# A feed-forward block with a conditioned layer norm: the norm by pairs of tiles, x split half an item ahead

## The chip, the cores and the metric

One core of one Trainium2 chip. Times are device microseconds of one execution. Engines by their names in the profile: PE is TensorE (PEld its weight loads), DVE VectorE, ACT ScalarE, POOL GpSimd, SP SyncE, whose queue issues the DMAs.

## The reference

```python
xr = x.reshape(4, 1024, 8, 128)                                  # x: (4, 1024, 1024) f32
h = gelu(einsum('btel,elf->btef', xr, W1) + b1)                  # W1: (8, 128, 512), exact gelu
y = (einsum('btef,efl->btel', h, W2) + b2).reshape(4, 1024, 1024)  # W2: (8, 512, 128)
eo = silu(emb) @ emb_W + emb_b                                   # emb: (4, 1024), emb_W: (1024, 2048)
scale, shift = split(eo[:, None, :], 2, axis=-1)
hn = layernorm(y, ln_g, ln_b) * (1.0 + scale) + shift            # over the 1024 features
out = x + silu(hn) @ out_W + out_b                               # out_W: (1024, 1024)
```

## The kernel before

Every matmul of weight is made of three in fp32r: each operand is split into a rounded part (`_hi`) and the rest (`_lo`), and hi x hi, lo x hi and hi x lo are added up in PSUM. For each such operand one engine rounds (a cast) and one subtracts.

**Stage A** runs over 32 items (`ORDER`, line 32): a feature group g of 8 and a token tile t of 1024 tokens. Groups 0 to 5 go through all four tiles each, groups 6 and 7 tile by tile. An item has four chunks c of 128 hidden features; m = 4n + c counts the chunks. `first(m)` (line 672) multiplies W1's chunk with x (x comes transposed as `xT`), six matmuls of 512 columns; ScalarE applies gelu into `g_raw`; ScalarE (c = 3, 0) or VectorE (c = 1, 2) rounds to `g_hi`, VectorE subtracts to `g_lo` (`split_gelu`, line 528); `second(m)` (line 686) adds W2's chunk into the item's y. TensorE's order is written out by hand: for each m, `first(m + 2)`, then `second(m)` (lines 733 to 769). The ring of two PSUM slots (`USES`, `SLOT`, `take`) is shared with small matmuls: eight embeddings of the condition (`embed`), their turning, and three steps of window 0's norm.

x of item n+1 is rounded by ScalarE at the start of item n (`round_x`) and its rest made by VectorE at c = 1 (`rest_x`, line 523), one chunk ahead of its first use at c = 2. The raw weights of both stages are rounded by ScalarE (`round_raw`, line 408) and subtracted by GpSimd (`low`, line 347). ScalarE stages y to SBUF (`stage_y`), SP stores it to `y_scratch`; VectorE adds it up over the groups into `acc` (`add_up`, line 540), from which the mean comes by one matmul with `ones`. SP's order in an item (lines 280 to 312): raw weights, emb_W, x of item n+2, then the store of y.

**Stage B** runs over 8 windows of 512 tokens. A window has four tiles of 128 tokens; a tile is 8 groups of six matmuls (`project`, line 771). Meanwhile the next window is normed (`window`, line 610): mean by a matmul of `acc`, centring on VectorE, squares on ScalarE, a tree of sums on VectorE, `variance` (four one-column fp32 matmuls), root on ScalarE, reciprocal of 4 columns, `spread` (four transposes) back over the features, the multiplication, silu on ScalarE with scale and bias, rounding and rest. `finish(q)` adds the tile's product to `res`, to which GpSimd has added out_b; SP stores it. Window 0 is normed inside stage A's last items, mostly on GpSimd (lines 362 to 376), and its silu stands behind stage A's last gelu (lines 467 to 478, and VectorE's lines 595 to 603).

Of the kernel before, what the change touches and what calls it, by code (L numbers as in the profile page):

```python
# [5 lines left out]
P = 128  # L6
# [5 lines left out]
BANK = 512  # L12
# [3 lines left out]
def cond_ffn_program(nc, x, xT, vectors, W1, W2, emb_W, out_W, out_b, out):  # L16
# [7 lines left out]
    TB = BANK  # L24
    NB = B * T // TB
    SB = TB // P
# [5 lines left out]
    ORDER = [(g, t) for g in range(G - 2) for t in range(NT)] + [(g, t) for t in range(NT) for g in (G - 2, G - 1)]  # L32
# [5 lines left out]
    Y0_ITEM = ITEM_OF[G - 1, 0]  # L38


    LOADS = [("W", 0), ("W", 1), ("W", 2), ("O", 0), ("O", 1), ("W", 3), ("O", 2), ("O", 3), ("W", 4), ("O", 4),
             ("W", 5), ("O", 5), ("W", 6), ("O", 6), ("W", 7), ("O", 7)]
    PREP_ITEM = [None, 0, 1, 2, 3, 5, 6, 7, 9, 11, 13, 15, 17, 19, 21, 22]
    LOAD_OF = {u: j for j, u in enumerate(LOADS)}
    PREP_AT = {n: j for j, n in enumerate(PREP_ITEM) if n is not None}
    EMB_ITEM = [5 + 2 * r for r in range(KE)]
    EMB_AT = {(n, 2): r for r, n in enumerate(EMB_ITEM)}
    TURN_AT = (21, 2)
    Y0_MEAN_AT = (Y0_ITEM + 2, 0)
    Y0_SQ_AT = [(Y0_ITEM + 2, 3), (Y0_ITEM + 3, 1), (Y0_ITEM + 3, 2), (Y0_ITEM + 4, 0)]  # L50
    Y0_VAR_AT = (Y0_ITEM + 4, 3)
    Y0_RSTD_AT = (Y0_ITEM + 5, 1)


    USES = [("S", 0), ("S", 1)]
    for m in range(M):
        at = divmod(m, C)
        if at in EMB_AT:
            USES.append(("E", EMB_AT[at]))
        if at == TURN_AT:  # L60
            USES.append(("F", 0))
        if at == Y0_MEAN_AT:
            USES.append(("M", 0))
        if at == Y0_VAR_AT:
            USES.append(("V", 0))
        if at == Y0_RSTD_AT:
            USES.append(("R", 0))
        if m + 2 < M:
            USES.append(("S", m + 2))
    SLOT = {u: j % 2 for j, u in enumerate(USES)}  # L70
    EARLIER = {u: USES[j - 2] for j, u in enumerate(USES) if j >= 2}
# [5 lines left out]

    y_scratch = nc.dram_tensor("y_scratch", [NB, P, G, TB], F32, kind="Internal").ap()

# [9 lines left out]
    with ExitStack() as ctx:  # L89
# [14 lines left out]
        acc = at("acc", [P, NT, TA], 64 * KB)  # L104
        S0 = 80 * KB
        ident = at("ident", [P, P], S0)
        ones = at("ones", [P, P], S0 + 512)
        cols = at("cols", [P, ROWS], S0 + 1024)
        stat = at("stat", [P, TB], S0 + 1536)
        emb_rows = at("emb_rows", [P, BANK], S0 + 3584)  # L110
        sq_sum = emb_rows
        cond_silu = at("cond_silu", [P, KE, 32], S0 + 5632)
        emb = at("emb", [P, NE, B], S0 + 6656)
        mod_a = at("mod_a", [P, B, G], S0 + 6912)
        mod_c = at("mod_c", [P, B, G], S0 + 7040)
        mod_t = at("mod_t", [P, B, G], S0 + 7168)
        eps = at("eps", [P, 1], S0 + 7296)
        std = at("std", [P, SB], S0 + 7328)
        rstd = at("rstd", [P, SB], S0 + 7360)
        R0 = S0 + 15 * 512  # L120


        yb0 = at("yb0", [P, G, TB], R0)
        emb_raw = at("emb_raw", [P, 2 * D], R0 + 16 * KB)
        wraw = at("wraw", [P, 2, 2 * FF], R0 + 24 * KB)
        squares = at("squares", [P, 4, TB], R0 + 24 * KB)
        xT_raw = at("xT_raw", [P, 2, TA], R0 + 32 * KB)
        xT_hi = at("xT_hi", [P, 2, TA], R0 + 40 * KB, F32R)
        xT_lo = at("xT_lo", [P, 2, TA], R0 + 48 * KB, F32R)
        g_raw = at("g_raw", [P, 2, TA], R0 + 56 * KB)  # L130
        g_hi = at("g_hi", [P, 2, TA], R0 + 64 * KB, F32R)
        g_lo = at("g_lo", [P, 2, TA], R0 + 72 * KB, F32R)
        W = at("W", [P, 3, 4, FF], R0 + 80 * KB, F32R)
        y_stage = at("y_stage", [P, 2, TA], R0 + 104 * KB)
        out_b_all = at("out_b_all", [P, D], R0 + 112 * KB)

        yb1 = at("yb1", [P, G, TB], R0 + 16 * KB)
        s_hi0 = at("s_hi0", [P, G, TB], R0 + 32 * KB, F32R)
        s_lo0 = at("s_lo0", [P, G, TB], R0 + 48 * KB, F32R)
        sq0 = at("sq0", [P, G, TB], R0 + 48 * KB)  # L140
        s_hi1 = at("s_hi1", [P, G, TB], R0 + 64 * KB, F32R)
        s_lo1 = at("s_lo1", [P, G, TB], R0 + 80 * KB, F32R)
        sq1 = at("sq1", [P, G, TB], R0 + 80 * KB)
        res = at("res", [P, 4, D], R0 + 96 * KB)
        yb = (yb0, yb1)
        s_hi = (s_hi0, s_hi1)
        s_lo = (s_lo0, s_lo1)
        sq = (sq0, sq1)
# [4 lines left out]
        ident_ready = sem("ident_ready")  # L153
        ones_ready = sem("ones_ready")
# [3 lines left out]
        w_hi_done = sem("w_hi_done")  # L158
        w_split0 = sem("w_split0")
# [6 lines left out]
        aw_hi_done = sem("aw_hi_done")  # L166
        pw_split = sem("pw_split")
# [694 lines left out]
```

## Time and profile before

| | us |
|---|---|
| median of 3 runs (790.39 to 793.78) | 792.9 |
| the profiled execution | 794.72 |
| its span, first to last instruction | 792.9 |
| PE busy | 751.7 (95%) |
| DVE busy | 489.3 (62%) |
| ACT busy | 418.1 (53%) |
| POOL busy | 165.6 (21%) |
| mean granted clock of TensorE | 0.982 |

Busy time is the time in which an engine has an instruction under way. The chain of the work that ended last goes to 78% through PE, to 11% through DVE and to 5% through ACT.

### The profile page before, as it was taken

Reading aid. Unit: us, or ns where it says so; the run is one execution under the profiler, and the core shown is the slowest. Engines: PE = TensorE matmul, PEld = TensorE weight load, DVE = VectorE, ACT = ScalarE, POOL = GpSimd, SP = SyncE. Lnnn points to the kernel's source line nnn. Section 1 sums busy time; section 2 is a strip of 40 time slices with the busy share of each in tenths; the row PEclk is TensorE's granted clock in tenths of the full one; section 3 lists DMA queues with packets and bytes.
Section 4 is the critical chain, followed back from the end, with each engine's and each line's share of the span. In section 5 each row is a group of like instructions: output and inputs, shape, how many; then the busy total and the mean of one; then the engine's idle time right before and its main releaser. Section 6 shows DMA issues by size and latency. Waiting matters only on the chain.

```text
span 792.9 us, 8091 instructions
## 1 busy us (share of the span) xinstructions
PE 751.7 (95%) x3252; PEld 597.4 (75%) x3252; DVE 489.3 (62%) x393; ACT 418.1 (53%) x413; POOL 165.6 (21%) x91
## 2 busy tenths in 40 slices
PE   6999999999999999996877999999999999999998
PEld 5777777777787777674655867888788888878886
DVE  6778778877877877766498256355444535554211
ACT  6877877777877777665652143334250423425000
POOL 1221211110101200335372112212221221121210
PEclk9999999999999999998989999999999999999999
DMA  5333554335543222511072243252423325212221
GB/s 214 119 120 134 169 175 153 136 137 186 186 158 109 107 77 83 213 53 54 26 292 106 80 139 127 107 212 89 176 107 136 129 107 212 99 61 107 106 80 53
DMA packets 33268, 101.75 MB, mean 128 GB/s; under 512 B 3024, under 2 KB 7120, under 8 KB 31056
## 3 DMA queue, kind: packets, MB, share of 16 engines
q1 hardware_dynamic: 32560, 100.73, 35.3%
q10 hardware_dynamic: 672, 0.52, 0.2%
q8 instruction: 25, 0.41, 0.2%
q14 instruction: 11, 0.09, 0.0%
HBM read 67.69 MB, written 33.55 MB: 128 GB/s over the span
## 4 chain that ended last, share of the span: by engine, by line
PE 78%; DVE 11%; ACT 5%; issue 4%; DMA 2%; POOL 1%; SPq 0%; ACTq 0%; DVEq 0%; POOLq 0%
PE psum L778 39%; PE psum L682 17%; PE psum L696 17%; DVE g_lo L537 4%; DVE xT_lo L525 2%; DVE g_hi L535 2%; PE psum L789 1%; ACT g_raw L400 1%; DMA xT_raw<-in_xT 1%; PE psum L711 1%; PE psum L822 1%; PE psum L704 1%; DVE s_hi L599 1%; ACT yb L470 1%; ACT xT_hi L392 1%
## 5 line engine op out<-in xcount | busy, mean ns | idle before, releaser
L537 DVE TENSOR_TENSOR g_lo<-g_raw,g_hi 128x1024 fp32r<-128x1024 f32 x128 | 178.3, 1393 | 74.1 <-ACT g_hi L406 71.9
L400 ACT ACTIVATE g_raw<-psum,cols 128x1024 f32<-128x1024 f32 x128 | 142.9, 1117 | 71.1 <-PE psum L682 69.8
L778 PE MATMUL psum<-oW_hi,s_hi 128*128 128x512 f32 x496 | 159.7, 403 | 3.7 <-DVE res L608 1.9
L778 PE MATMUL psum<-oW_hi,s_lo 128*128 128x512 f32 x496 | 155.2, 394 | 1.6 <-DVE s_lo L601 1.6
L778 PE MATMUL psum<-oW_lo,s_hi 128*128 128x512 f32 x496 | 154.3, 393 | 0.0
L682 PE MATMUL psum<-xT_hi,W 128*128 128x512 f32 x508 | 140.0, 398 | 5.0 <-ACT g_raw L400 2.6
L696 PE MATMUL psum<-g_hi,W 128*128 128x512 f32 x512 | 140.2, 396 | 0.0
L381 POOL TENSOR_TENSOR res<-res,out_b_all 128x1024 f32<-128x1024 f32 x32 | 79.0, 2472 | 281.6 <-DMA res<-in_x 281.6
L682 PEld LDWEIGHTS psum<-xT_hi,W 128*128 128x128 f32 x508 | 95.7, 191 | 33.4 <-issue 9.3
L696 PEld LDWEIGHTS psum<-g_hi,W 128*128 128x128 f32 x512 | 97.6, 191 | 22.1 <-DVE g_hi L535 0.5
L778 PEld LDWEIGHTS psum<-oW_hi,s_hi 128*128 128x128 f32 x496 | 93.4, 191 | 26.8 <-issue 4.1
L778 PEld LDWEIGHTS psum<-oW_hi,s_lo 128*128 128x128 f32 x496 | 94.2, 190 | 21.9 <-DVE s_lo L601 2.0
L778 PEld LDWEIGHTS psum<-oW_lo,s_hi 128*128 128x128 f32 x496 | 94.1, 190 | 20.1
L682 PE MATMUL psum<-xT_lo,W 128*128 128x512 f32 x254 | 82.4, 406 | 13.4 <-DVE xT_lo L525 13.4
L608 DVE TENSOR_TENSOR res<-psum,res 128x1024 f32<-128x1024 f32 x31 | 37.7, 1220 | 88.3 <-PE psum L778 88.3
L487 ACT ACTIVATE sq<-yb 128x2048 f32<-128x2048 f32 x14 | 26.9, 1919 | 120.8 <-DVE yb L617 120.8
L696 PE MATMUL psum<-g_lo,W 128*128 128x512 f32 x256 | 80.2, 395 | 2.2 <-DVE g_lo L537 2.2
L406 ACT CAST g_hi<-g_raw 128x1024 fp32r<-128x1024 f32 x64 | 67.2, 1050 | 22.4 <-PE psum L696 22.3
L470 ACT ACTIVATE yb<-yb,mod_c,mod_a 128x512 f32<-128x512 f32 x64 | 46.9, 804 | 47.4 <-DVE yb L633 47.4
L682 PEld LDWEIGHTS psum<-xT_lo,W 128*128 128x128 f32 x254 | 46.4, 191 | 31.2 <-DVE xT_lo L525 22.4
L535 DVE CAST g_hi<-g_raw 128x1024 fp32r<-128x1024 f32 x64 | 47.2, 738 | 22.7 <-ACT g_raw L400 17.0
L696 PEld LDWEIGHTS psum<-g_lo,W 128*128 128x128 f32 x256 | 48.5, 190 | 13.8 <-DVE g_lo L537 3.5
(83 smaller groups left out, 554.3 us busy)
## 6 DMA issues: line engine op xcount, KB each, us to landing
y_scratch<-y_stage SPq DMA_DIRECT2D x32, 512.0 KB, 2.9
res<-in_x SPq DMA_DIRECT2D x32, 512.0 KB, 3.9
xT_raw<-in_xT SPq DMA_DIRECT2D x31, 512.0 KB, 4.4
out<-res SPq DMA_DIRECT2D x31, 512.0 KB, 2.8
yb<-y_scratch SPq DMA_DIRECT2D x7, 2048.0 KB, 9.5
emb_raw<-in_emb_W SPq DMA_DIRECT2D x8, 1024.0 KB, 7.7
wraw<-in_out_W SPq DMA_DIRECT2D x16, 256.0 KB, 3.7
wraw<-in_W SPq DMA_DIRECT2D x14, 256.0 KB, 3.6
```

Of the source, the lines that this page charges most:

```text
L381: nc.gpsimd.tensor_tensor(res[:, q % 4], res[:, q % 4], out_b_all[:], ALU.add).then_inc(res_biased, 1)
L400: nc.scalar.activation(g_raw[:, m % 2], ring(("S", m)), ACT.Gelu, bias=cols[:, R_B1 + k:R_B1 + k + 1]).then_inc(gelu_done, 1)
L406: nc.scalar.copy(g_hi[:, m % 2], g_raw[:, m % 2]).then_inc(ghi_act, 1)
L470: return nc.scalar.activation(yb[s][:, g], yb[s][:, g], ACT.Silu, scale=mod_a[:, b, g:g + 1], bias=mod_c[:, b, g:g + 1])
L487: nc.scalar.activation(sq[s][:, half], yb[s][:, half], ACT.Square).then_inc(squared, 1)
L525: nc.vector.tensor_tensor(xT_lo[:, n % 2], xT_raw[:, n % 2], xT_hi[:, n % 2].bitcast(F32), ALU.subtract).then_inc(xlo_done, 1)
L535: nc.vector.tensor_copy(g_hi[:, m % 2], g_raw[:, m % 2]).then_inc(ghi_dve, 1)
L537: nc.vector.tensor_tensor(g_lo[:, m % 2], g_raw[:, m % 2], g_hi[:, m % 2].bitcast(F32), ALU.subtract).then_inc(glo_done, 1)
L608: nc.vector.tensor_tensor(res[:, q % 4], proj(q), res[:, q % 4], ALU.add).then_inc(out_ready, 1)
L682: mm = nc.tensor.matmul(ps[:, half], W[:, g % 3, w, cut], v[:, n % 2, half], start=(k == 0), stop=(k == 2))
L696: mm = nc.tensor.matmul(y_psum(n)[:, half], W[:, g % 3, w, cut], v[:, m % 2, half], start=(c == 0 and k == 0), stop=(c == C - 1 and k == 2))
L778: mm = nc.tensor.matmul(proj(q)[:, half], v[:, g, cut], w[:, g, half], start=(g == 0 and k == 0), stop=(g == G - 1 and k == 2))
```

## The change

- The norm works on pairs of token tiles (256 tokens, `NP` = 16 pairs) in place of windows of 512, two pairs ahead, with three y buffers (`load_y`, 1 MB each).
- `acc`, `add_up`, `variance` and `spread` are gone. Mean and variance come from a tree of sums over the groups of y or of its squares, made on VectorE; the sum is split high and low (`sum_hi`, `sum_lo`) and summed over the partitions by two fp32r matmuls with a 128x128 of 1/D, which leave it in every partition (`row_sum`). The reciprocal then has 256 columns.
- Pair 0's norm is spread by hand over items 24 to 30 of stage A, on VectorE and ScalarE. Its silu is computed as v(1 + tanh v) with v half the argument (`halve_y0`, `tanh_y0`, `silu_y0`). Pair 1's mean is in item 31.
- Items: groups 5, 6 and 7 are now the ones that go tile by tile, so tile 0's y is complete with item 22. Four weight slots (`WS`) in place of three.
- x of item n+2 is rounded at c = 2 and its rest made at c = 3 of item n. SP issues x's load first in an item; the y store stands right before it.
- Both steps of the weights' split are VectorE's (`split_raw`); GpSimd has only `ident` and the `res` additions left.
- The small matmuls of stage A use a bank of the free y slot (`small`) in place of the ring.
- Two fp32 matmuls on zeros run on TensorE before the first weights are there.

```diff
-    ORDER = [(g, t) for g in range(G - 2) for t in range(NT)] + [(g, t) for t in range(NT) for g in (G - 2, G - 1)]
+    LATE = range(G - 3, G)
+    ORDER = [(g, t) for g in range(G - 3) for t in range(NT)] + [(g, t) for t in range(NT) for g in LATE]
...
+    SPLIT_ITEM = [None, 0, 1, 2, 3, 5, 7, 8, 9, 11, 12, 13, 14, 15, 17, 19]
+    EMB_ITEM = [4 + 2 * r for r in range(KE)]
+    TURN_ITEM = 20
+    Y0_MEAN_AT = (25, 1)
+    Y0_VAR_AT = (27, 1)
+    Y1_MEAN_AT = (31, 3)
...
         def _(sp):
+                if n + 2 < N:
+                    sp.wait_ge(xlo_done, n + 1)
+                    load_x(n + 2)
...
                 if n == Y0_ITEM + 1:
+                    sp.wait_ge(emb_chunk, KE)
                     for s in range(2):
+                        sp.wait_ge(y_stored[s], 16 * len(range(s, Y0_ITEM + 1, 2)))
+                    for p in range(3):
+                        load_y(p)
...
         def _(act):
+                if c == 2 and n + 2 < N:
+                    round_x(n + 2)
+                if (n, c) == (28, 0):
+                    root(0, total[:])
+                    nc.scalar.preload_act_table(ACT.Gelu)
                 if m + 2 < M:
                     gelu(m + 2)
+                if (n, c) == (25, 3):
+                    square(0, 0)
+                if (n, c) == (26, 0):
+                    square(0, 1)
+                if (n, c) == (28, 3):
+                    act.wait_ge(mod_step, 7)
+                    halve_y0(0)
+                    halve_y0(1)
+                if (n, c) == (29, 0):
+                    halve_y0(2)
+                    halve_y0(3)
+                if (n, c) == (29, 1):
+                    tanh_y0(0)
+                if (n, c) == (29, 3):
+                    round_y0(0)
+                    halve_y0(4)
+                    halve_y0(5)
+                if (n, c) == (30, 0):
+                    halve_y0(6)
+                    halve_y0(7)
+                    tanh_y0(1)
+                if (n, c) == (30, 2):
+                    round_y0(1)
...
         def _(dve):
+            def split_raw(j, h):
+                raw = wraw[:, j % 2, half]
+                nc.vector.tensor_copy(hi, raw).then_inc(w_rounded, 1)
+                nc.vector.tensor_tensor(lo, raw, hi.bitcast(F32), ALU.subtract).then_inc(w_split, 1)
...
+                if c == 3 and n + 2 < N:
+                    rest_x(n + 2)
+                if m + 2 < M:
+                    split_gelu(m + 2)
+                if c in (0, 2) and n in SPLIT_AT:
+                    split_raw(SPLIT_AT[n], c // 2)
...
+            for i in range(NP):
+                p, ahead = i + 1, i + 2
+                if p < NP:
+                    invert(p, rstd_ps)
+                    norm(p, 0, rstd_ps)
+                    norm(p, 1, rstd_ps)
                 if i > 0:
+                    finish(2 * i - 1)
+                if ahead < NP:
+                    mean_sum_first(ahead)
+                    mean_sum_rest(ahead)
+                    mean_split_up(ahead)
+                if p < NP:
+                    rest_s(p, 0)
+                if ahead < NP:
+                    centre(ahead, 0, mean_ps)
+                    centre(ahead, 1, mean_ps)
+                if p < NP:
+                    rest_s(p, 1)
+                finish(2 * i)
+                if ahead < NP:
+                    var_sum_first(ahead)
+                    var_sum_rest(ahead)
+                    var_split_up(ahead)
...
         def _(pe):
+            def row_sum(ps):
+                nc.tensor.matmul(ps, ones_r[:], sum_hi[:], start=True, stop=False)
+                return nc.tensor.matmul(ps, ones_r[:], sum_lo[:], start=False, stop=True)
...
+            pe.wait_ge(emb_copied, 1)
+            for j in range(2):
+                nc.tensor.matmul(psum[:, 7], emb_rows[:, 0:P], emb_rows[:], start=True, stop=True)
...
+            for i in range(NP):
+                ahead = i + 2
+                for t in range(2):
...
+                        project(q, g)
+                        if i == 0:
+                            if (t, g) == (0, 4):
+                                var_of(1)
+                            if (t, g) == (1, 1):
+                                mean_of(ahead)
+                        elif ahead < NP:
+                            if (t, g) == (0, 0) and i == 1:
+                                var_of(2)
+                            if (t, g) == (0, 6):
+                                mean_of(ahead)
+                            if (t, g) == (1, 6):
+                                var_of(ahead)
```

## Rows read from the trace of the kernel before

**Rows 1.** Three stretches; stretch: length, busy us (instructions), clock, DMA share, GB/s.
```profile
110.40:317.50 207.10, 205.08 (x907) 159.85 (x906) 163.07 (x155) 158.89 (x159) 25.35 (x16) 1.00 0.40 138
317.50:424.30 106.80, 83.83 (x313) 62.87 (x312) 76.14 (x58) 61.41 (x63) 50.46 (x27) 0.90 0.33 123
489.90:720.30 230.40, 230.40 (x1032) 188.14 (x1031) 114.12 (x71) 81.31 (x75) 48.18 (x21) 1.00 0.35 128
```

**Rows 2.** Timeline of ACT: stagings of items 0, 26 and 31; start, duration.
```profile
23.16 1.12 ACT L423 ACTIVATE y_stage<-psum,cols 128x1024 f32<-128x1024 f32 x1
...
327.58 1.11 ACT L423 ACTIVATE y_stage<-psum,cols 128x1024 f32<-128x1024 f32 x1 [0.24 <-PE psum L696]
...
406.30 1.09 ACT L423 ACTIVATE y_stage<-psum,cols 128x1024 f32<-128x1024 f32 x1
```

**Rows 3.** The chain in stage A, 110 to 162 us; start, duration, what.
```profile
116.70 1.36 PE psum L696 x6
118.06 1.36 PE psum L682 x6
...
123.50 1.00 PE psum L704 x8
```

**Rows 4.** The chain in stage B, 510 us on.
```profile
517.16 0.86 PE psum L822 x2
...
528.94 1.03 PE psum L711 x8
...
535.53 0.44 PE psum L717 x4
535.97 27.23 PE psum L778 x120
```

**Rows 5.** Waits: waiter, line, waited for: us in total, times, longest.
```profile
PE psum L682 <- DVE xT_lo L525: 13.4, 11, 4.4
```

**Rows 6.** Timeline of POOL and DVE near 27 us.
```profile
26.81 1.29 POOL L348 TENSOR_TENSOR W<-wraw,W 128x512 fp32r<-128x512 f32 x1 [2.86 <-ACT W L415]
...
26.99 2.20 DVE L537 TENSOR_TENSOR g_lo<-g_raw,g_hi 128x1024 fp32r<-128x1024 f32 x1
...
29.11 1.21 DVE L525 TENSOR_TENSOR xT_lo<-xT_raw,xT_hi 128x1024 fp32r<-128x1024 f32 x1
```

**Rows 7.** Timeline of the start: chunk 2's gelu, and item 1's low part.
```profile
13.01 1.11 ACT L400 ACTIVATE g_raw<-psum,cols 128x1024 f32<-128x1024 f32 x1
...
18.28 0.73 PE L682 MATMUL psum<-xT_lo,W 128*128 128x512 f32 x2 [0.91 <-DVE xT_lo L525]
```

**Rows 8.** Groups by line and shape; count, busy us, mean ns, idle before.
```profile
L406 ACT CAST g_hi<-g_raw 128x1024 fp32r<-128x1024 f32 x64 | 67.2, 1050 | 22.4 <-PE psum L696 22.3
...
L535 DVE CAST g_hi<-g_raw 128x1024 fp32r<-128x1024 f32 x64 | 47.2, 738 | 22.7 <-ACT g_raw L400 17.0 <-PE psum L696 5.6
...
L548 DVE SCALAR_TENSOR_TENSOR acc<-psum,cols,acc 128x1024 f32<-128x1024 f32 x28 | 35.7, 1277 | 0.0
...
L488 ACT ACT_TABLE_LOAD x7 | 9.0, 1283 | 0.1
...
L415 ACT CAST W<-wraw 128x512 fp32r<-128x512 f32 x14 | 8.6, 614 | 0.0
...
L624 DVE TENSOR_TENSOR stat<-sq 128x512 f32<-128x512 f32 x7 | 4.8, 692 | 0.2
...
L627 DVE RECIPROCAL rstd<-std 128x4 f32<-128x4 f32 x7 | 1.2, 178 | 11.4 <-ACT std L490 11.4
...
L510 DVE CAST W<-wraw 128x512 fp32r<-128x512 f32 x2 | 0.8, 424 | 2.7 <-DMA wraw<-in_W 2.7
```

**Rows 9.** SP's timeline at 227 us, landings of `xT_raw`, and the page's DMA issues.
```profile
227.04 0.43 SPq L256 DMA_DIRECT2D xT_raw<-in_xT  x1
...
DMA to landing us min/median/max: 3.6/4.1/9.1
...
yb<-y_scratch SPq DMA_DIRECT2D x7, 2048.0 KB, 9.5
```

**Rows 10.** The chain's last matmuls.
```profile
778.76 10.89 PE psum L789 x48
```

More of the change, by code:

```diff
@@ L126, in cond_ffn_program @@
[L126 to L144, printed above, removed]
@@ new lines, in _ @@
+            for q in range(QN):
+                if q < QN - 1:
+                    sp.wait_ge(out_ready, q + 1)
+                    sp.dma_start(out_rows[q], res[:, q % 4]).then_inc(out_stored[q % 4], 16)
+                else:
+                    for h in range(2):
+                        half = slice(h * BANK, (h + 1) * BANK)
+                        sp.wait_ge(out_ready, QN + h)
+                        sp.dma_start(out_rows[q, :, half], res[:, q % 4, half]).then_inc(out_stored[q % 4], 16)
+                if q % 2 == 0 and q // 2 + 4 < NP:
+                    p = q // 2 + 4
+                    sp.wait_ge(slo_done, 2 * (p - 3) + 2)
+                    load_y(p)
+                if q >= 1 and q + 3 < QN:
+                    sp.wait_ge(out_stored[(q - 1) % 4], 16 * ((q - 1) // 4 + 1))
+                    load_res(q + 3)
@@ new lines, in centre, with var_sum_first @@
+            def centre(p, h, mean):
+                dve.wait_ge(mean_done, p + 1)
+                part = yb[p % 3][:, half_of(h)]
+                nc.vector.tensor_tensor(part, part, mean.unsqueeze(1).to_broadcast([P, HG, TP]), ALU.subtract
+                                        ).then_inc(centred, 1)
+            def var_sum_first(p):
+                dve.wait_ge(squared, 2 * p + 2)
+                nc.vector.tensor_tensor(sq[:, 0:4], sq[:, 0:4], sq[:, 4:8], ALU.add).then_inc(var_tree, 1)
@@ new lines, in invert, with norm, silu_y0 @@
+            def invert(p, rstd):
+                dve.wait_ge(std_done, p + 1)
+                nc.vector.reciprocal(rstd, std[:]).then_inc(rstd_done, 1)
+            def norm(p, h, rstd):
+                dve.wait_ge(rstd_done, p + 1)
+                part = yb[p % 3][:, half_of(h)]
+                nc.vector.tensor_tensor(part, part, rstd.unsqueeze(1).to_broadcast([P, HG, TP]), ALU.mult
+                                        ).then_inc(normed, 1)
+            def silu_y0(h):
+                dve.wait_ge(y0_tanh, h + 1)
+                part = yb0[:, half_of(h)]
+                nc.vector.scalar_tensor_tensor(part, sq[:, half_of(h)], 1.0, part, ALU.add, ALU.mult
+                                               ).then_inc(y0_silu, 1)
@@ new lines, in _ @@
+                if (n, c) == (28, 3):
+                    norm(0, 1, total[:])
+                if (n, c) == (29, 2):
+                    silu_y0(0)
+                if (n, c) == (30, 0):
+                    rest_s(0, 0)
+                if (n, c) == (30, 1):
+                    silu_y0(1)
+                if (n, c) == (30, 3):
+                    rest_s(0, 1)
+                if (n, c) == (31, 0):
+                    mean_sum_first(1)
+                if (n, c) == (31, 1):
+                    mean_sum_rest(1)
+                    mean_split_up(1)
```

666 lines of the change are left out of this document (281 added, 385 removed).

## The prediction

> **What bounds the kernel now.** I read the stretches first: TensorE's busy time in each, and its clock. From 110 to 317 us the PE is busy 205.08 of 207.10 us, and from 490 to 720 us all of 230.40 us; from 317.5 to 424.3 us it is busy for 83.8 of 106.8 us at a granted clock of 0.90 [rows 1]. So TensorE is the bound except in the middle. The chain gives its pace: six matmuls, one call of `first` or `second` or one group of `project`, take 1.36 us in stage A [rows 3], and 120 of stage B take 27.23 us, 0.2269 us each, so 1.361 us for six [rows 4]. The kernel has 256 sixes in stage A and 256 in stage B: 696.8 us of the 792.9 us span. The rest, 96 us, is what can be won.
>
> Where it lies: stage A's items. An item is eight sixes, 10.89 us. From the staging of item 0 (23.16 us) to that of item 26 (327.58 us) an item took 304.42/26 = 11.71 us; the last five took 78.7 us where 51.7 us of matmuls stand [rows 2]. That is 21 us in the first part (8 of it for the condition's eight embeddings, 1.00 us each [rows 3]) and 27 us in the second. 10 us lie before item 0's staging (ten sixes are 13.6 us), and 38 us behind item 31's: 16.3 for seven windows of norm matmuls, 3.3 behind the last matmul, 18.6 of stalls at the start of stage B. The waits show the cause in the first part: TensorE for `xT_lo` 13.4 us [rows 5]; and where GpSimd runs at the same time, a `g_lo` of VectorE takes 2.20 us instead of the 1.22 that a subtraction of this size takes by itself [rows 6]. That delays `xT_lo`, which stands one chunk ahead of its use. In stage B a window of four tiles has 192 project matmuls (43.57 us) and 0.86 + 1.03 + 0.44 = 2.33 us of norm matmuls [rows 4].
>
> **The change, part by part.** T is the time at which TensorE begins an item; the order in an item is first, second, four times, 1.36 us each.
>
> *Start.* Two warm-up matmuls and a reordered VectorE. Before, the fifth call of `first` got its low part at 18.28 us [rows 7]. After, VectorE does for it: the split of chunk 2 (gelu ready at 14.12 us [rows 7], cast 0.74, low part 1.22), then half a weight split (0.42 + 0.69 [rows 8]), then `rest_x(1)` (1.22): 18.4 us. The warmed clock wins about 1 us earlier, but this wait swallows it. I take item 0 staged at 23.3 us; -1 to +1.
>
> *VectorE in stage A.* Gone: `add_up` (1.28 an item) [rows 8] and GpSimd's 30 half splits, with the 2.20 us cases. New: both halves of each weight split on VectorE. A full item is now 4 x 1.22 + 2 x 0.74 + 1.22 (`rest_x`) + 2 x (0.42 + 0.69) = 9.8 us, and 0.69 for an embedding, against 10.89 (11.9 with embedding): it fits. Order matters too: chunk 4n+4's low part ends at T+11.1, the half split at T+12.2, `rest_x(n+2)` at T+13.3 and chunk 4n+5's cast and low part at T+14.0 and T+15.2; TensorE wants these at T+14.96 and T+15.9. 0.7 us are left, the thinnest cover of the change; where embedding and split meet (items 8, 12, 14) I book 0.3 us in all. ScalarE loses 30 casts of 0.61 us and has 4 x 1.12 + 2 x 1.05 + 1.05 + 1.12 = 8.7 of 10.89 us.
>
> *x half an item ahead.* `xT_hi` and `xT_lo` of item n+2 are made in item n, so TensorE's 13.4 us of waits go. What is late next is the load: issued at about T+1.6 (behind the y store, now ahead of the weight and embedding loads), wanted by ScalarE at T+6.6. 5.0 us against a landing of 4.1 us in the median and 9.1 at most; the 9.1 goes with an issue at 227.04 us behind weights and emb_W [rows 9]. So nothing in an ordinary item. In item 23, however, the three 1 MB loads of y are new on this queue: 2 MB took 9.5 us [rows 9], so 3 MB some 14 us at that rate, perhaps 11, from T+4; they end at T(24)+4 to +8, with the y store and x of item 24 behind them. x comes 2 to 6 us late, ScalarE and VectorE have 1 to 2 us in hand there. I take 2 us lost; 0 to 5.
>
> *Stage A's sum.* From item 0's staging to the end of A stand 246 sixes, 334.8 us. Embeddings 8 x 1.15 = 9.2 (1.00 each plus a part of a refilled weight load; 8.0 at least). The turn 0.7. Three row sums 0.9.
>
> *Pair 0's norm in items 24 to 30* replaces the tail in which `second`, the POOL chain and window 0 waited for each other. TensorE no longer waits on it; only its load on ScalarE and VectorE counts. 24 to 27 add at most 3.1 us of VectorE a item, which had 3.4 free. Item 28 adds on ScalarE two table loads (1.28 each [rows 8]) and a root (0.5) before a gelu: the gelu ends at T+5.4, wanted at T+5.44. Items 28 to 30 then add 8 scalings of 256 columns (0.40 each, from 0.61 for 512 and 1.05 for 1024), two tanh and two roundings (1.05 each). Item 28 is 12.5 us of ScalarE and item 29 12.4 us, 3.1 us over two items' TensorE time; and a scaling stands behind `normed`, a rounding behind `silu_y0`, with the next gelu queued behind both. Followed, chunk by chunk, that costs TensorE 3 to 4.5 us. I take 3.8; 1 to 8.
>
> A ends at 23.3 + 334.8 + 9.2 + 0.7 + 0.9 + 0.3 + 2 + 3.8 = 375.0 us. Before, its last staging began at 406.3 us, and stalls went on behind it: the slow stretch reaches to 424.3 us [rows 1, 2].
>
> *Stage B.* 256 sixes, 348.4 us. Row sums: two fp32r matmuls of 256 columns take the place of mean, variance and spread. No row has one. From below: half of 0.2269 each, 0.23 us a sum; from above, the fp32 mean of before, 512 columns in 0.86 us: 256 columns twice are 0.43 each at its pace if both passes are needed, 0.57 with a restart of the next weight load. I take 0.30, near the fp32r row, since `ones_r` and the sums are fp32r. 29 of them in B: 8.7 us (6.7 to 16.5), where the seven windows had 16.3.
>
> Does the rest hide? VectorE a pair (22.4 us of TensorE): 2 norm, 2 centre, 2 `finish`, 2 `rest_s` and 2 first tree steps of 1024 columns, 12.3 us; two second steps (0.69), two third (0.42), two split-ups (0.3 + 0.42), 3.7 us; the reciprocal. It now has 256 columns, the rows only 4, 0.178 us [rows 8]; at one column a cycle it is 0.42. Beyond that it is bounded above by the 1024-column row, 1.22; I take 0.5. Sum 16.5 us, plus about 2 us of meeting GpSimd's two res adds. It fits with 4 us over. In order: invert and norms end at 2 us of the window, `finish` 3.3, the mean's split 7, TensorE asks at 9.5; variance's split at 18, asked for at 20.9. Hidden. In the first window they are tight (asked for at 6.8 us after B's start, ready at 6.7): 1.5 us booked, 0 to 4.
>
> The Trainium skill speaks against my reciprocal: "VectorE: DVE Perf Modes" (the 8-slice pipeline) says that it repeats its divide 8 times per element. By that 256 columns would be an estimated 2.3 us, the window of VectorE 18.3 us, still hidden, and the sum 2 us more, in the first window.
>
> **The sum.** 375.0 + 348.4 + 8.7 + 1.5 and the tail behind the last matmul, 792.93 - 789.65 = 3.3 us [rows 10], is a span of 736.9 us. The profiled execution ran 794.72 us for a span of 792.93, 1.8 more, and lies 1.8 above the median of 792.9: in terms of the median the two cancel. **737 us.**
>
> **Rivals.** (1) *VectorE or ScalarE becomes the bound of a full item in A.* The 0.7 us of cover is gone if each semaphore step costs a little more than I read. Eleven split items at 1 us each, four late items at 2 more: 737 + 11 + 8 = 756. For: the thinnest margin in the change. Against: back-to-back VectorE instructions start about 0.08 us before the last ends. 0.12.
> (2) *B's norm chain is late for TensorE's fixed places.* If reciprocal and meetings with GpSimd take 4 us more, the mean is late at (0, 6) by 1 us in each of 14 windows: 737 + 14 = 751. For: one chain, in order, through three engines. Against: 2.5 us spare. 0.10.
> (3) *Tanh isn't with Gelu in the loaded table.* A load there and back before each of two tanh, 2 x 2 x 1.28 = 5.1 us on ScalarE in items 29 and 30, where it has nothing over: 742. The diff puts no load there, and every load in the trace of before stands at a `preload` line; that is against it. The Trainium skill, "ScalarE: Activation LUTs" (table sets), lists tanh with exp and with sigmoid, not with gelu, and would have it so. 0.08.
> (4) *Slower: x lands late in every item.* If 1 KB pieces of the y store and the shorter lead make each x land as late as the worst before, 9.1 us, it is 4.1 us behind its 5.0 us, 2.4 beyond what ScalarE has over, 30 times: 737 + 72 = 809. It beats the gain from a landing of some 8.5 us on. Against: x is now issued before the big loads, and 2.5 MB an item move at 210 GB/s. 0.03.
> (5) *Nothing in the tail is won*: the pair norm stalls `second` as before, 27 us in the last items return: 764. 0.04.
> The forecast holds the remaining 0.63.
>
> **Range.** All unknowns good (no stalls, sums at 0.23, embeddings 1.00): 737 - 7.6 - 2.2 - 1.2 = 726; two of them good, 729. Above, sums at 0.57 and rivals 2 and 1: to 756. 729 to 756. Faster by over 0.5% (about what can be told from no change here) 0.95, the same 0.02, slower 0.03.
>
> **What would show it.** Stagings of item 0 and 27 some 307 us apart or less (27 x 10.89 + 9.2 + 2 + 1.6); no wait for `xT_lo`; all `g_lo` near 1.22 us; GpSimd idle before its res adds; a clock of 1.00 from 20 us on; ScalarE's waits in items 28 to 30 for `normed` and `silu_y0`, with TensorE waiting for g_raw or `g_lo` there; B's windows of two tiles at 22.4 us. Wrong it would be if x's landing exceeds 6 us in many items, if a row sum takes over 0.5 us, or if VectorE fills over 95% of an item.

## The result, and the profile after

| | before | after |
|---|---|---|
| median, us | 792.6 | 750.8 (749.7 to 754.2) |
| profiled execution, us | 794.7 | 751.7 |
| its span | 792.9 | 749.9 |
| ratio to before, 95% interval | | 0.948 (0.944 to 0.952) |

The kernel before ran again in the same round, hence 792.6 and not 792.9. The change makes the kernel 5% faster, and its time is 14 us above the forecast of 737, inside the range of 729 to 756. The page of the kernel after gives busy us, share of the span and instructions of each engine:

```profile
PE 729.4 (97%) x3208; PEld 588.0 (78%) x3208; DVE 549.6 (73%) x618; ACT 457.6 (61%) x502; POOL 78.5 (10%) x38
```

VectorE has 60 us more work than before, GpSimd 87 us less, TensorE 22 us less. Where the forecast was missed shows in the stretches. The columns are those of [rows 1]: length, busy us of each engine with its instructions, clock, DMA share, GB/s.

```profile
110.00:290.00 180.00, 179.88 (x806) 143.38 (x805) 136.54 (x159) 134.66 (x126) 0.00 (x0) 1.00 0.48 161
290.00:340.00 50.00, 45.41 (x188) 36.73 (x187) 35.33 (x39) 35.47 (x35) 0.00 (x0) 0.93 0.23 78
340.00:380.00 40.00, 37.66 (x156) 27.84 (x154) 32.07 (x30) 34.77 (x39) 0.00 (x0) 1.00 0.24 73
380.00:430.00 50.00, 43.26 (x185) 34.93 (x186) 43.43 (x47) 26.96 (x34) 12.04 (x5) 0.97 0.35 131
490.00:700.00 210.00, 210.00 (x944) 174.37 (x943) 160.67 (x180) 105.47 (x138) 44.99 (x20) 1.00 0.38 136
```

In the first row 0.1 of 180 us are idle, before it was 2.0 of 207 [rows 1]. Stage B from 490 us on is full too. What is lost lies between 290 and 430 us: 13.7 us without a matmul, and two stretches with a granted clock below 1.00, the first of which no engine's load explains: VectorE is 71% busy from 290 to 340 us. From 380 to 430 us it is 87% busy, part of it in operations that GpSimd stretches (below). The waits (waiter, line, waited for: us in total, times, longest) name who ends it:

```profile
PE psum L753 <- DVE sum_lo L548: 7.8, 4, 3.5
...
PE psum L753 <- DVE sum_lo L571: 3.8, 2, 2.2
...
PE psum L713 <- DVE xT_lo L498: 1.6, 1, 1.6
```

L753 is the row sum on TensorE, L548 and L571 the low part of the mean's and of the variance's sum. The row of `xT_lo` is what is left of the 13.4 us in [rows 5]; it is item 1's at the start. The timeline of item 25, VectorE first, then TensorE (start, duration, line, operation, tile, and in brackets the idle time before it and who ended it):

```profile
296.76 0.69 DVE L508 CAST g_hi<-g_raw 128x1024 fp32r<-128x1024 f32 x1
297.49 1.23 DVE L510 TENSOR_TENSOR g_lo<-g_raw,g_hi 128x1024 fp32r<-128x1024 f32 x1
298.63 0.29 DVE L546 CAST sum_hi<-total 128x256 fp32r<-128x256 f32 x1
298.95 0.42 DVE L548 TENSOR_TENSOR sum_lo<-total,sum_hi 128x256 fp32r<-128x256 f32 x1
```

```profile
296.47 0.61 PE L729 MATMUL psum<-g_lo,W 128*128 128x512 f32 x2
299.52 0.55 PE L753 MATMUL psum<-sum_hi,ones_r 128*128 128x256 f32 x1 [2.44 <-DVE sum_lo L548]
299.87 0.41 PE L754 MATMUL psum<-sum_lo,ones_r 128*128 128x256 f32 x1
300.08 1.91 PE L713 MATMUL psum<-xT_hi,W 128*128 128x512 f32 x4
```

TensorE arrives at the row sum at 297.1 us. VectorE has the split of the sum behind the cast and low part of a gelu that TensorE wants only after the row sum, and finishes it at 299.37. TensorE stands for 2.44 us, and the four matmuls behind the stop take 1.91 us where the usual is 1.07: half pace, the 1.2 GHz level. The same comes at (27, 1) with 2.16 us and at (31, 3) with 3.48 us.

The row sum in stage B's first window stops for 1.61 us too (395.15 us). There VectorE's split takes six times its 0.42 us, while GpSimd works from 392.45 us on:

```profile
392.55 2.54 DVE L571 TENSOR_TENSOR sum_lo<-total,sum_hi 128x256 fp32r<-128x256 f32 x1
```

The terms of the sum beside the trace, in us. The last column is the version e5_gate, told below.

| | forecast | after | e5_gate |
|---|---|---|---|
| item 0 staged | 23.3 | 22.0 | 22.3 |
| from there to item 24's staging | 271.3 | 272.4 | 272.5 |
| from there to the end of A | 80.4 | 91.0 | 80.1 |
| stage B up to the last matmul | 358.6 | 361.3 | 358.4 |
| tail | 3.3 | 3.2 | 3.2 |
| span | 736.9 | 749.9 | 736.4 |

### The profile page after: what moved, and what is told of

It reads as the page before. It is cut to its first block, busy times and chain, and to the rows that moved or that the text cites. A ratio compares the mean times of both kernels' runs of the same rounds, so it can differ in the third digit from the quotient of the medians.

```text
span 749.9 us, 8247 instructions
## 1 busy us (share of the span) xinstructions
PE 729.4 (97%) x3208; PEld 588.0 (78%) x3208; DVE 549.6 (73%) x618; ACT 457.6 (61%) x502; POOL 78.5 (10%) x38
## 4 chain that ended last, share of the span: by engine, by line
PE 84%; DVE 7%; ACT 5%; issue 2%; DMA 1%; SPq 0%; ACTq 0%; DVEq 0%
PE psum L818 42%; PE psum L713 19%; PE psum L729 19%; DVE g_lo L510 2%; ACT g_raw L347 2%; PE psum L830 1%; ACT g_hi L353 1%; PE psum L739 1%; PE psum L753 1%; DMA xT_raw<-in_xT 1%; DVE yb L581 1%; DVE g_hi L508 1%; DMA cols<-in_vectors 1%; ACT y_stage L360 1%; PE psum L754 1%
## 5 line engine op out<-in xcount | busy, mean ns | idle before, releaser
L510 DVE TENSOR_TENSOR g_lo<-g_raw,g_hi 128x1024 fp32r<-128x1024 f32 x128 | 156.8, 1225 | 82.9 <-ACT g_hi L353 80.4
L818 PE MATMUL psum<-oW_hi,s_hi 128*128 128x512 f32 x496 | 153.7, 391 | 0.0
L818 PE MATMUL psum<-oW_hi,s_lo 128*128 128x512 f32 x496 | 153.2, 390 | 0.0
L818 PEld LDWEIGHTS psum<-oW_hi,s_hi 128*128 128x128 f32 x496 | 91.6, 189 | 17.3
L713 PE MATMUL psum<-xT_lo,W 128*128 128x512 f32 x254 | 79.3, 394 | 1.6 <-DVE xT_lo L498 1.6
L729 PE MATMUL psum<-g_lo,W 128*128 128x512 f32 x256 | 80.1, 394 | 0.1
L451 ACT ACTIVATE yb<-yb,mod_c,mod_a 128x256 f32<-128x256 f32 x120 | 62.4, 590 | 26.8 <-DVE yb L581 26.8
L576 DVE RECIPROCAL psum<-std 128x256 f32<-128x256 f32 x15 | 26.4, 1761 | 52.9 <-ACT std L377 52.9
L377 ACT ACTIVATE std<-psum,eps 128x256 f32<-128x256 f32 x15 | 7.2, 477 | 93.5 <-PE psum L754 93.5
L365 ACT ACTIVATE sq<-yb 128x1024 f32<-128x1024 f32 x32 | 34.0, 1063 | 40.6 <-DVE yb L554 39.6
L713 PEld LDWEIGHTS psum<-xT_lo,W 128*128 128x128 f32 x254 | 48.2, 190 | 12.1 <-DVE xT_lo L498 2.0
```

Of the source, the lines that this page charges most:

```text
L365: nc.scalar.activation(sq[:, half_of(h)], yb[p % 3][:, half_of(h)], ACT.Square).then_inc(squared, 1)
L451: nc.scalar.activation(yb[p % 3][:, g], yb[p % 3][:, g], ACT.Silu, scale=mod_a[:, b, g:g + 1], bias=mod_c[:, b, g:g + 1]).then_inc(silu_do ...
L510: nc.vector.tensor_tensor(g_lo[:, m % 2], g_raw[:, m % 2], g_hi[:, m % 2].bitcast(F32), ALU.subtract).then_inc(glo_done, 1)
L576: nc.vector.reciprocal(rstd, std[:]).then_inc(rstd_done, 1)
L713: mm = nc.tensor.matmul(ring(m)[:, half], W[:, g % WS, w, cut], v[:, n % 2, half], start=(k == 0), stop=(k == 2))
L729: mm = nc.tensor.matmul(y_psum(n)[:, half], W[:, g % WS, w, cut], v[:, m % 2, half], start=(c == 0 and k == 0), stop=(c == C - 1 and k == 2))
```

## Experiments

**Is it the place of the row sums?** The theory at this point was that both row sums of pair 0 stand one chunk too early in TensorE's order, and that pair 1's mean is begun too late on VectorE. The rival was the clock: the stops are short, and what counts is the half pace behind them. Four kernels ran beside each other, the first of them the changed kernel once more.

> The changed kernel once more, as the measure for the runs beside it: 750 us, with TensorE's three stops in front of the row sums of items 25, 27 and 31 (2.4, 2.2 and 3.5 us) where they were.

Measured: 749.2 us (747.2 to 751.9), ratio 0.945 (0.941 to 0.949). The three stops are there with 2.57 us and about the same two others, but in this execution TensorE kept its pace behind the first two:

```profile
300.83 0.36 PE L753 MATMUL psum<-sum_hi,ones_r 128*128 128x256 f32 x1 [2.57 <-DVE sum_lo L548]
301.02 0.28 PE L754 MATMUL psum<-sum_lo,ones_r 128*128 128x256 f32 x1
301.14 1.09 PE L713 MATMUL psum<-xT_hi,W 128*128 128x512 f32 x4
```

So the same stop lowers the granted clock in one execution and not in another (from 290 to 340 us it is 1.00 here, 0.93 in the profile after). From item 24's to item 28's staging this execution takes 52.4 us, the other 55.4: so the half pace behind the first two stops is worth 2.9 us. Up to item 31's staging 2.3 of it are left (89.3 against 91.6), because here the half pace behind the third stop begins at the row sum itself.

Then the places alone:

```diff
-    Y0_MEAN_AT = (25, 1)
-    Y0_VAR_AT = (27, 1)
+    Y0_MEAN_AT = (25, 2)
+    Y0_VAR_AT = (27, 2)
```

> The row sums of pair 0's mean and variance stand one chunk later in TensorE's order, (25, 2) and (27, 2). Theory: the stops come only from the fixed place, which asks for sum_lo 13.6 us after item 24's start while VectorE has it after 16.1. One chunk later it is asked for at 16.3. Items 25 and 27 fall from 15.2 and 15.1 us to 11.3, so the time falls by 7 to 8 us, to 742 to 743. Rival: ScalarE and VectorE have no time to spare in items 24 to 28, and the stop is only where that shows; then the same time is lost behind it, at g_hi or g_lo, and less than 2 us come back (748 or more).

Measured: 742.8 us (742.1 to 743.2), ratio 0.936 (0.934 to 0.939), 6.5 us below a0_again, near the theory's 7 to 8 and far from the recorded rival's less than 2. Both stops are gone: the stagings of items 24 and 28 are 47.2 us apart, where a0_again has 52.4 and the profile after 55.4. One `sum_lo` stop is left in stage A, that of (31, 3), again 3.48 us.

Next, pair 1's mean tree half an item earlier on VectorE as well:

```diff
+                if (n, c) == (30, 2):
+                    mean_sum_first(1)
                 if (n, c) == (30, 3):
                     rest_s(0, 1)
-                if (n, c) == (31, 0):
-                    mean_sum_first(1)
-                if (n, c) == (31, 1):
                     mean_sum_rest(1)
+                if (n, c) == (31, 0):
                     mean_split_up(1)
```

> Beside e1's edit, pair 1's sums for the mean are made one to three chunks earlier on VectorE, so that sum_lo is there when TensorE reaches (31, 3). Theory: the 3.5 us stop there and about 1.5 us at half clock behind it go too, and stage B's first row sums, which hang on the same chain, wait less: 12 to 15 us below the changed kernel, 735 to 738. Rival: items 30 and 31 are bound by ScalarE's gelus behind the halved and tanh work, and VectorE's tree now pushes g_lo back by its own length; then no more than 1 us below e1.

Measured: 746.4 us (745.3 to 746.9), ratio 0.941 (0.938 to 0.943), slower than e1_places by 3.7. The stop at (31, 3) did go, and stage B began at 375.35 us instead of 379.28. But the next row sum, pair 1's variance in the first window of B, was then late, by more than was won: in e1_places it had not waited. The timelines of GpSimd, VectorE and TensorE in this kernel:

```profile
376.94 10.95 POOL L328 TENSOR_TENSOR res<-res,out_b_all 128x1024 f32<-128x1024 f32 x4 [375.49 <-DMA res<-in_x]
```

```profile
380.46 2.76 DVE L563 TENSOR_TENSOR sq<-sq 128x512 f32<-128x512 f32 x1
383.26 2.44 DVE L565 TENSOR_TENSOR total<-sq 128x256 f32<-128x256 f32 x1
385.73 2.31 DVE L569 CAST sum_hi<-total 128x256 fp32r<-128x256 f32 x1
388.08 0.42 DVE L571 TENSOR_TENSOR sum_lo<-total,sum_hi 128x256 fp32r<-128x256 f32 x1
```

```profile
388.56 0.58 PE L753 MATMUL psum<-sum_hi,ones_r 128*128 128x256 f32 x1 [6.23 <-DVE sum_lo L571]
```

GpSimd's four additions of x and bias run back to back for 10.95 us. Within them a VectorE addition of 512 columns takes 2.76 us (0.69 elsewhere), one of 256 columns 2.44 (0.42), a cast of 256 columns 2.31 (0.29): each sits out one GpSimd addition, and the first one behind GpSimd's end is back at 0.42. In e1_places the four additions came two and two (from 377.74 and from 385.22 us), and the small steps of the tree, 383.63 to 385.56 us, passed between them. So a third mechanism was at work that neither theory nor rival held.

The clock rival was tried by giving TensorE unread matmuls ahead of the row sums of the changed kernel (10, 9 and 15 of them, on a free bank), so that it is busy until `sum_lo` is there:

```diff
                 if (n, c) == Y0_MEAN_AT:
                     pe.wait_ge(y_staged, n)
                     pe.wait_ge(ones_ready, 1)
+                    fill(n, 10)
                     pe.wait_ge(mean_split, 2)
```

> Before each of the three row sums TensorE runs matmuls whose results nobody reads (10, 9 and 15 of 512 columns, 2.3, 2.0 and 3.4 us), about as long as it stood still there. Theory: the stop itself costs 8.1 us and remains; but behind each stop a call of six matmuls took 1.9 to 2.5 us in place of 1.36, with a granted clock of 0.91 to 0.98 in the stretches there, some 4 us in all. With the engine busy the clock stays at its upper level and these 4 us come back: 746. Rival: the slow matmuls behind a stop are data or weight waits, not the clock; then nothing comes back, 750 or a little more.

Measured: 751.3 us (750.9 to 752.1), ratio 0.947 (0.945 to 0.950): nothing came back. The pace behind all three places is full in its profile, and from item 24's to item 31's staging it takes 88.5 us, 0.8 less than a0_again, which lost its pace at the third stop alone. But in B's first window the variance was late by 5.2 us, at a clock of 0.83 from 380 to 400 us: GpSimd's additions fell on the split of the sum, a cast of 2.31 us (0.29) and a subtraction of 2.44 (0.42). Matmuls without an idle time ahead of them kept the full pace, which speaks against the recorded rival (data or weights late behind a stop), but in one execution only. What the fillers alone are worth can't be read from this run; removing the stops is worth 6.5 us, and that is the way that pays.

**Does GpSimd hold VectorE?** The third mechanism got a run of its own. To e3_both comes one thing: GpSimd's additions wait.

```diff
+                if q == 0:
+                    pool.wait_ge(mean_split, 6)
+                if q == 2:
+                    pool.wait_ge(var_split, 6)
```

> The two earlier places and the earlier mean tree as in e3_both, and GpSimd's four res additions before stage B are held until VectorE has split the mean's sum (first two) and the variance's sum (last two) of pair 1. Theory (a GpSimd addition holds VectorE's SBUF operations, up to 2.76 us for a 128x512 addition instead of 0.69): with GpSimd idle during the variance tree of pair 1, its operations return to 0.69, 0.42 and 0.29 us, the wait of 6.2 us on sum_lo goes to about 0 to 1 us, TensorE keeps 2.4 GHz behind it, and the span is 736 to 738 us, 6 to 8 below e3_both. Rival (VectorE is slow there for a reason of its own, such as its queue of psum evictions): the wait stays near 6 us and the span near 745. Second rival (the held additions come late for the first windows of B, which need res): the wait goes, but TensorE or ScalarE waits 2 to 5 us for res later, span 740 to 743.

Measured: 738.6 us (738.1 to 739.1), ratio 0.932 (0.929 to 0.935), span 736.4. VectorE's tree in this kernel, and the row sum that waits for it:

```profile
379.62 0.69 DVE L567 TENSOR_TENSOR sq<-sq 128x512 f32<-128x512 f32 x1
380.35 0.43 DVE L569 TENSOR_TENSOR total<-sq 128x256 f32<-128x256 f32 x1
380.81 0.29 DVE L573 CAST sum_hi<-total 128x256 fp32r<-128x256 f32 x1
381.13 0.43 DVE L575 TENSOR_TENSOR sum_lo<-total,sum_hi 128x256 fp32r<-128x256 f32 x1
```

```profile
381.67 0.33 PE L757 MATMUL psum<-sum_hi,ones_r 128*128 128x256 f32 x1
```

All four are at their usual length, and the row sum has no idle time before it. The only difference to e3_both is that GpSimd stands still, so the hold by GpSimd is shown. Its price here is 7.8 us between the medians and 8.5 between the two profiled spans, the half pace behind the stop of 6.23 us included. The second rival, additions that come late for the first windows, doesn't show in the time. The Trainium skill has this as a rule ("SBUF — State Buffer", Who interferes with whom): VectorE with two SBUF inputs, or in a two-port mode, as casts can be, shares one port pair with GpSimd, and whoever starts first has it for the whole instruction. The trace agrees, and also in what it says of an operation with only one SBUF input. Further on in the same kernel, one that reads PSUM runs at its usual 1.21 us within two GpSimd additions:

```profile
390.97 1.21 DVE L558 TENSOR_TENSOR yb<-yb,psum 128x1024 f32<-128x1024 f32 x1
```

```profile
390.06 6.65 POOL L332 TENSOR_TENSOR res<-res,out_b_all 128x1024 f32<-128x1024 f32 x2 [388.60 <-DVE sum_lo L552]
```

Over the whole changed kernel it is the same: VectorE's subtractions of the mean, of which one operand lies in PSUM, average 1.22 us (L554, 32 of them), while the first additions of the variance's tree, with both in SBUF, average 1.32 (L559, 16 of the same size) and reach 2.91.

**What won stage A's ordinary items?** Three things changed there at once: the place of x's split, the engine of the weights' split, and that `add_up` is gone and the small matmuls have a bank of their own. The first two were put back one at a time. First the split of x:

```diff
-                if m == 0:
-                    round_x(1)
-                if c == 2 and n + 2 < N:
-                    round_x(n + 2)
+                if c == 0 and n + 1 < N:
+                    round_x(n + 1)
```

(and `rest_x` likewise, from c = 3 to c = 1).

> The change with the splitting of x put back to where the kernel before had it (item n+1's x rounded in the first quarter of item n and its rest in the second), everything else as changed. My prediction priced a late xT_lo by the wait rows of before (13.4 us in all) and the contention of GpSimd and VectorE. Theory: most of what stage A won comes from the split half an item ahead, so this kernel is 15 to 23 us slower than the changed one (765 to 772). Rival: what won was taking GpSimd off the path of g_lo, and with that VectorE has room for x in either place; then it is less than 8 us slower (750 to 757).

Measured: 767.0 us (766.0 to 767.7), ratio 0.968 (0.965 to 0.970). The wait is back, larger than in [rows 5]:

```profile
PE psum L709 <- DVE xT_lo L496: 18.8, 16, 3.0
```

From item 0's to item 24's staging this kernel takes 287.0 us, the changed one 272.4, the one before 282.2. An item with a weight split takes 12.17 us, one without split and embedding 11.13, against 10.88. So with x in its old place the rest of the change makes these items 4.8 us slower than before; half an item more for x turned it around. The 12.17 us of the items with a split point at the weights' split on VectorE, but no kernel ran with x in its old place and that split on GpSimd.

Second, the low parts of the weights back to GpSimd:

> The change with the low parts of the weights (from the second load on) subtracted on GpSimd again, as in the kernel before, instead of on VectorE. In the kernel before g_lo took 2.20 us beside GpSimd's work, in the changed one it takes 1.23 us. Theory: the held VectorE operations fall in few items (those with a weight load) and x is split half an item ahead, so they cost 0 to 3 us. Rival: contention between GpSimd and VectorE was the main loss of stage A, and the kernel is 10 to 15 us slower than the changed one.

Measured: 748.3 us (747.7 to 749.6), ratio 0.944 (0.942 to 0.947), no difference to the changed kernel. The groups of VectorE from 25 to 280 us (count, busy us, mean ns, idle before) show that the hold is there all the same, a cast at 955 ns instead of 688, `g_lo` at 1338 instead of 1225 and `xT_lo` at 1316 instead of 1218, 24 us in all:

```profile
L523 DVE TENSOR_TENSOR g_lo<-g_raw,g_hi 128x1024 fp32r<-128x1024 f32 x91 | 121.7, 1338 | 51.7 <-ACT g_hi L365 49.1
L521 DVE CAST g_hi<-g_raw 128x1024 fp32r<-128x1024 f32 x45 | 43.0, 955 | 0.0
L511 DVE TENSOR_TENSOR xT_lo<-xT_raw,xT_hi 128x1024 fp32r<-128x1024 f32 x22 | 29.0, 1316 | 0.0
```

Most items still take 10.88 us, and from item 0's to item 24's staging it is 272.2 us against 272.4. With x ahead, VectorE has the room, and which engine subtracts the weights makes no difference. So the gain of these items (282.2 to 272.4 us) hangs on x's lead: without it they take 287.0. The prediction had put the 2.20 us of [rows 6] beside it as a cause. With x ahead such a hold costs nothing; what it cost while x stood one chunk ahead of its use was not run, and the third thing was not put back.

**How thin is stage B's cover?** The reciprocal came out at 1.76 us, 3.5 times the 0.5 of the prediction. So it was doubled, with the first result unread:

```diff
                 if p:
+                    nc.vector.reciprocal(total[:], std[:])
```

> The reciprocal of every pair but the first is made twice (the first result is not read), 1.76 us more of VectorE in every window of stage B of 22.27 us. Theory: the profile of the changed kernel shows sum_lo of the mean 1.8 us and of the variance 2.4 us ahead of TensorE's row sums, and the doubled reciprocal lies behind the variance, ahead of the next mean, so it eats at most the 1.8 us: steady windows stay at 22.27 us, the first windows lose 2 to 4 us, in all 751 to 756. Rival (VectorE bounds stage B once 1.8 us are added, each of 15 windows loses 1 us or more): 765 or more.

Measured: 755.6 us (751.9 to 757.7), ratio 0.953 (0.949 to 0.956). The chain of this kernel from 551 us on (start, duration, what):

```profile
551.42 0.12 PE psum L755
551.54 0.12 PE psum L756
551.66 10.91 PE psum L820 x48
562.57 0.12 PE psum L755
```

Steady windows stay at 22.3 us. VectorE has the mean's `sum_lo` at 562.20 us and TensorE asks at 562.57: 0.4 us left of 1.8. The first windows pay: the row sums there wait 3.60, 1.04 and 2.41 us, where the changed kernel has 1.61, 1.04 and 0.81, and from the row sum of (31, 3) to the fifth one behind it stand 57.6 us instead of 50.8. That is 7 us: 3.6 of longer waits, as expected (2 to 4), and over 3 of half pace behind the stops of 3.60 and 2.41 us, which nobody had booked (granted clock 0.83 from 396 to 406 us, 0.87 from 427 to 440). The profiled execution is the slowest of its four (751.9 to 757.7 us); the median lies 4.8 us above the changed kernel's, inside the 751 to 756 expected.

**What is left, and two small parts.** The last four ran beside each other, e5_gate first.

> The kernel of e5_gate once more, as the measure for the three beside it: 738 to 739 us, span 736 to 737, stage A ending at 375.0 us of its profile.

Measured: 738.9 us (738.1 to 739.5), ratio 0.932 (0.931 to 0.934).

> On top of e5_gate: ScalarE scales two more quarters of pair 0's tile before it rounds the first half (it waited 1.41 us for that half's silu), and VectorE's rest_s of pair 0's second half moves from item 30 to item 31, ahead of which the cast of g_hi then comes (TensorE waited 1.83 us for g_hi at 369.3 us). Theory: what is left of pair 0's cost in items 28 to 31 is order, not load, so 1.5 to 2.5 us come back: span 734 to 735. Rival (ScalarE's and VectorE's load there is what counts): within 0.5 us of e5_again.

```diff
                 if (n, c) == (30, 3):
-                    rest_s(0, 1)
                     mean_sum_rest(1)
...
+                if (n, c) == (31, 1):
+                    rest_s(0, 1)
...
-                    round_y0(0)
                     halve_y0(4)
                     halve_y0(5)
+                    round_y0(0)
```

Measured: 737.3 us (737.1 to 737.8), ratio 0.931 (0.929 to 0.932), 1.7 us below e5_again. Stage B begins at 372.73 us, 2.4 earlier than there (375.1), but half of that goes again in B's first window, most of it at the row sum that now comes before its sum is split:

```profile
380.63 0.39 PE L758 MATMUL psum<-sum_hi,ones_r 128*128 128x256 f32 x1 [0.92 <-DVE sum_lo L575]
```

The theory of order holds, with 1.7 us of its 1.5 to 2.5. This is the fastest version: 55 us below the kernel before, 12 to 14 below the changed one, and level with the forecast.

> e5_gate without the two warm-up matmuls on zeros ahead of TensorE's first real one. The staging of item 0 ended at 23.16 us in the kernel before and at 21.96 in the changed one; I had given the start nothing. Theory now: the warm-up lifts TensorE's clock sooner, so without it item 0 is staged 1.0 to 1.3 us later and everything behind it. Rival (the gain at the start came from the split of x ahead or the earlier weight): staging within 0.2 us of e5_again.

Measured: 739.1 us (738.9 to 740.6), ratio 0.933 (0.932 to 0.934), the same as e5_again. The trace is clearer than the time. The fifth call of `first`, which waits for item 1's low part, without the warm-up here, and with it (e5_again) in the second fence:

```profile
18.20 0.73 PE L717 MATMUL psum<-xT_lo,W 128*128 128x512 f32 x2 [1.31 <-DVE xT_lo L502]
```

```profile
17.28 0.73 PE L717 MATMUL psum<-xT_lo,W 128*128 128x512 f32 x2 [1.56 <-DVE xT_lo L502]
```

Item 0 is staged at 23.09 us without and 22.15 with it. Of this 0.9, 0.4 was given back in item 24, where ScalarE waited 0.7 us for x in e5_again and 0.2 in u5_cold. And the warm-up does not always take: in a0_again, e1_places, u2_xlate and u6_tables TensorE's first two real matmuls ran at half pace behind it (1.22 us instead of 0.73), and item 0 was staged at 23.1, 22.6, 22.3 and 23.5. So the expected 1.0 to 1.3 us came out as 0.9 at the first item and as nothing that the time shows.

> e5_gate with two table loads of ScalarE (Silu's, then Gelu's again; 1.28 us each by the profile's rows) ahead of each of the two tanh operations of pair 0, items 29 and 30: what a silu by its own table would need there. Only the loads are added; what they load is not used between them. Theory (ScalarE sets the pace of items 28 to 30): 5.1 us of loads less the 1.4 and 0.3 us that ScalarE waited for silu anyway: 3 to 4 us slower than e5_again. Rival (the 3.2 us lost there are VectorE's or the order's): under 1.5 us.

```diff
+                nc.scalar.preload_act_table(ACT.Silu)
+                nc.scalar.preload_act_table(ACT.Gelu)
                 nc.scalar.activation(sq[:, half_of(h)], yb0[:, half_of(h)], ACT.Tanh).then_inc(y0_tanh, 1)
```

Measured: 743.9 us (743.3 to 744.8), ratio 0.939 (0.937 to 0.940), 5.0 above e5_again. The stagings of items 28 to 30 are 16.22 and 13.22 us apart instead of 13.54 and 10.65, 5.3 us for 5.1 us of loads. My 3 to 4 had taken ScalarE's waits for the silu as slack; they stayed, since `silu_y0` needs the tanh and came later with it. ScalarE's load does set the pace there, and tanh keeps 5 us out of it.

## Why the prediction was off by 14 us

**Right: what bounds and what is won.** Sixes of 1.36 us throughout, items of 10.88 us, 12.11 with an embedding (1.23 where 1.15 was booked), no wait for x in ordinary items, stage B's windows at 22.28 us. Of the 96 us beyond the sixes the change takes 42, and with two other places, an earlier tree and a gate on GpSimd 54.

**The step that failed: "TensorE no longer waits on it; only its load on ScalarE and VectorE counts."** It was said of pair 0's norm in items 24 to 30. The prediction followed items 28 to 30 chunk by chunk and got 3.8 us, and for stage B it set "asked for" against "ready" for both sums. For items 25, 27 and 31 it did neither, and took 0.3 us a row sum, the matmuls alone. The rows to do it were there: TensorE reaches (25, 1) two sixes into the item, and VectorE splits the sum behind the cast and low part of that item's chunk 1. The three stops measured 2.44, 2.16 and 3.48 us, 8.1 in all, with some 3 us of half pace behind them, against 0. e1_places and e5_gate show it by taking them away: the stretch from item 24's staging to the end of A goes from 91.0 to 83.9 us without the first two and to 80.1 without all three, where the sum had 80.4.

**Right in sum, wrong in terms.** Even the 80.1 is partly luck. I had 2 us for a late x in item 24, and it cost 0.0 to 0.4: in the profile after x landed 5.1 us from its issue, the three loads of y in 5.7, 7.8 and 9.9 us. Items 28 to 30 took 3.2 us more of TensorE than their sixes (forecast 3.8; their stagings lie further apart, since ScalarE comes to them late), but item 31, for which I had nothing, 2.8 more in e5_gate, 1.8 of them a wait for `g_hi`, which VectorE has behind the earlier tree. Where embedding and split meet the items took 1.0, not 0.3. The start gave 1.0 to 1.3 us, not nothing: I held the wait for item 1's low part fixed at 18.4 us, but VectorE's chain ahead of it hangs on gelu and so on TensorE, and moved along with it (u5_cold).

**Stage B.** A row sum costs 0.23 us (its two matmuls 0.11 and 0.12 us of the chain), the lower bound and not the 0.30; over 29 of them 2 us better. The reciprocal, above my upper bound of 1.22:

```profile
L576 DVE RECIPROCAL psum<-std 128x256 f32<-128x256 f32 x15 | 26.4, 1761 | 52.9 <-ACT std L377 52.9
```

The bound was no bound: a reciprocal is no addition, and the one row of it had 4 columns, nearly all start-up (0.178 us, where four columns at the pace of the long one are 0.03). By the Trainium skill ("VectorE: DVE Perf Modes", the 8-slice pipeline), which gives the divide a repeat count of 8, I had estimated 2.3 us; that was nearer than mine, but 0.5 us too long. The trace has a column at 6.3 ns, six times an addition's 1.0 and not eight times. In steady windows it is hidden all the same, as the sum said it would be; in the first ones it counts, with the hold by GpSimd that I had as "about 2 us of meeting" without a place. After: 2.7 us above the forecast for B. e5_gate is on it, but by two errors that cancel: the row sums are 2 us cheaper, and the first windows lose about 3 us where 1.5 were booked.

**The rivals.** (1) A full item bound by VectorE: no; 10.88 us, and even 24 us of held VectorE in u3_pool change nothing. (2) The norm chain late for fixed places was the right mechanism at the wrong end. I put it at (0, 6) in each window, where there are 1.8 us to spare, even with the reciprocal at 1.76; it struck where pair 0 and 1 are fitted into stage A and the first windows. (3) Tanh needs no load of its own: ScalarE's table loads in the trace after are those of the `preload` lines alone. Its price of 5.1 us was right (u6_tables, 5.0). The Trainium skill ("ScalarE: Activation LUTs", table sets) doesn't name tanh in gelu's set; here it runs between gelus without a load. (4) x late in every item: landings are 3.6 to 6.4 us, 4.6 in the median. (5) Nothing in the tail won: half true. From item 26's staging to item 31's it is 65.4 us, before 78.7 [rows 2], so 13 of the 27 us are won, and in e5_gate 19.

## What to carry to other kernels

When work is written by hand between the instructions of the bounding engine, list every place where that engine asks and when the helper engine has it, not only where the load is highest. Here a stop of 2 us cost 2 us, or nearly 4 when the clock fell behind it, and a place one chunk later cost nothing. And put a GpSimd elementwise operation where VectorE has PSUM operands to read or nothing urgent: the earlier tree of e3_both lost more to it (3.7 us net) than it won.

## What the runs showed of the hardware that I had not expected

- Back-to-back GpSimd additions of 1024 columns stretched VectorE's small SBUF operations four- to eightfold, each to about a whole GpSimd instruction (0.69 to 2.76, 0.42 to 2.44, 0.29 to 2.31 us).
- A reciprocal of 128x256 takes 1.76 us, one of 128x4 0.18 [rows 8]: 6.3 ns a column, against 1.0 of an addition (1.22 us for 1024, 0.69 for 512).
- TensorE behind the same stop of about 2.5 us ran on at its full pace in one execution and at half pace in another; behind warm-up matmuls on zeros it ran its first two real ones at half pace in 4 of 12 profiled executions, and in part in a fifth (u3_pool, 0.99 us). The changed kernel spreads over 747 to 754 us; without the stops it is 738.1 to 739.5. That the pace behind the stops makes that spread fits the two profiles (2.9 us behind the first two stops), and is not shown beyond them.
